# Attention on one NeuronCore: row maxima spread through DRAM by two DMAs instead of by TensorE transposes and ScalarE copies

## What is computed

```
# layer 0
xn  = group_norm(x) * gn_w + gn_b
q, k, v = split(qkv_w @ xn + qkv_b)
a   = softmax_over_keys(q . k / sqrt(64)) @ v        # per image and head, 2304 x 2304
h   = proj_w @ a + proj_b + x
# layer 1
q, k = [h, position embedding] @ Wq, Wk ;  v = h @ Wv
out = softmax_over_keys(q . k / sqrt(64)) @ v @ Wout + bout + h
```

## Time and profile before

| | |
|---|---|
| median of three runs | 4245.89 us |
| the profiled execution | 4246.06 us |
| its span in the trace | 4244.3 us |
| granted TensorE clock, mean | 0.992 |
| busy: TensorE, VectorE, ScalarE, GpSimd | 4090.6, 3200.4, 2775.9, 1408.4 us |
| attention of layer 0 and 1, first scores to about the last block | 408 to 1990 us, 2510 to 4100 us |
| DMA: bytes, mean rate | 208.42 MB, 49 GB/s |

### The profile page before, as it was taken

One profiled execution on the slowest core, in us unless ns is written; L12 is line 12 of the kernel. 1 busy time (PEld: TensorE's weight loads), 2 busy tenths in 40 slices (PEclk: granted clock), 3 DMA queues, 4 the chain that ended last, 5 costly groups with the idle time before them and its releaser, 6 DMA issues. The chain is left out here.

```text
span 4244.3 us, 88521 instructions
## 1 busy us (share of the span) xinstructions
PE 4090.6 (96%) x30024; PEld 1908.3 (45%) x30024; DVE 3200.4 (75%) x4032; ACT 2775.9 (65%) x3557; POOL 1408.4 (33%) x572
## 2 busy tenths in 40 slices
PE   7999899999999999998999989999999999999989
PEld 4554344444444444444555544444444444444445
DVE  3111899999999999997322239999999999999962
ACT  1112888888888888885000018888888888888840
POOL 0000344444444444443100004444444444444420
PEclk9999999999999999999999999999999999999999
DMA  4112000101000000011323220101000000000116
GB/s 175 74 74 93 10 27 19 37 13 32 20 28 22 22 24 24 26 49 53 117 100 126 97 95 9 30 19 33 19 28 24 22 22 26 24 20 30 41 45 215
DMA packets 157933, 208.42 MB, mean 49 GB/s; under 512 B 9008, under 2 KB 144304, under 8 KB 156848
## 3 DMA queue, kind: packets, MB, share of 16 engines
q1 hardware_dynamic: 137712, 179.28, 12.8%
q10 hardware_dynamic: 20160, 28.32, 1.8%
HBM read 113.19 MB, written 94.37 MB: 49 GB/s over the span
## 5 line engine op out<-in xcount | busy, mean ns | idle before, releaser
L589 POOL TENSOR_TENSOR prob<-prob,mx 128x1056 f32<-128x1056 f32 x564 | 1387.4, 2460 | 2627.5 <-DVE prob L589 2627.5
L753 ACT ACTIVATE prob<-psum_att 128x768 f32<-128x768 f32 x1728 | 1364.5, 822 | 951.7 <-PE psum_att L683 538.0
L683 PE MATMUL psum_att<-qst,kst 64*128 64x384 f32 x6912 | 1289.0, 505 | 30.6 <-DMA kst<-qk_scratch 18.0
L769 ACT ACTIVATE prob<-prob 128x1152 f32<-128x1152 f32 x1152 | 1291.2, 1172 | 17.3 <-POOL prob L589 15.1
L858 DVE TENSOR_TENSOR run<-psum_att,run 128x768 f32<-128x768 f32 x1344 | 1233.8, 950 | 36.1 <-PE psum_att L683 34.6
L694 PE MATMUL psum_att<-prob,vst 128*32 128x384 f32 x13824 | 1242.1, 491 | 0.7 <-ACT prob L769 0.5
L683 PEld LDWEIGHTS psum_att<-qst,kst 64*128 64x128 f32 x6912 | 623.6, 188 | 534.0 <-ACT prob L753 101.4
L589 DVE TENSOR_TENSOR prob<-prob,mx 128x1248 f32<-128x1248 f32 (+1 forms) x576 | 850.7, 1478 | 0.0
L694 PEld LDWEIGHTS psum_att<-prob,vst 128*32 128x32 f32 x13824 | 394.6, 109 | 755.3 <-issue 703.7
L870 DVE TENSOR_TENSOR two_tiles<-prob 128x768 f32<-128x768 f32 x564 | 565.3, 1002 | 1.1 <-ACT prob L769 1.1
L309 PE MATMUL psum<-xc_l,wq 128*128 128x384 f32 x1536 | 504.6, 490 | 9.3 <-DVE xc_l L382 4.4
(11 more groups left out here) (55 smaller groups left out, 1593.9 us busy)
## 6 DMA issues: line engine op xcount, KB each, us to landing
qk_scratch<-qk_l SPq DMA_DIRECT2D x48, 768.0 KB, 3.5
v_scratch<-vo_l SPq DMA_DIRECT2D x24, 768.0 KB, 3.5
qst<-qk_scratch SPq DMA_DIRECT2D x96, 192.0 KB, 2.4
kst<-qk_scratch SPq DMA_DIRECT2D x96, 192.0 KB, 2.4
vst<-v_scratch SPq DMA_DIRECT2D x96, 192.0 KB, 2.5
att_scratch<-ob ACTq DMA_DIRECT2D x96, 192.0 KB, 1.9
attc_l<-att_scratch SPq DMA_DIRECT2D x24, 768.0 KB, 5.7
x_sb<-in_x SPq DMA_DIRECT2D x8, 1152.0 KB, 14.0
```

The source lines that it names most:

```text
L589: return engine.tensor_tensor(x, x, m, ALU.subtract)
L683: mm = nc.tensor.matmul(psum[:, 2 * k + e, 0:CH], kst[rows, (3 * c + k) * P:(3 * c + k + 1) * P], qst[par][rows, :], start=True, stop=True ...
L753: nc.scalar.activation(prob[par][:, :, s, :], s_banks(k)[:, :, 0:CH], ACT.Copy).then_inc(copied, 1)
L769: nc.scalar.activation(x, x, ACT.Exp, scale=SCALE).then_inc(exp_done, 1)
```

## The change

The six broadcasting transposes and the three copies of a block go. In their place SyncE stores `mcol` to a DRAM scratch `max_scratch` (2 parities x 2 heads x 3 x 128 values; in DRAM the six values of a partition lie apart, so that each 4-byte value is a piece of its own), waits for the store, and loads the 768 values into all 128 partitions of `mx` (3 KB each). VectorE's and GpSimd's first subtraction of a block waits for that load (`mx_in`). Besides: `turn` stands behind the scores of c = 0, not ahead of them; `reduce` waits no more for scores; `pair_tiles` is done for the group 11 back at a group's start, not for the group 10 back at its end; the loops of SyncE are written out so that the first pair of heads is apart.

```diff
-SHIFT_LAG, EXP_LAG, PAIR_LAG, PV_LAG = 8, 9, 10, 11
-TURN_AT, BROADCAST_AT = 0, 1
+SHIFT_LAG, EXP_LAG, PAIR_LAG, PV_LAG = 8, 9, 11, 11
+TURN_AT = 0
...
+            def spread_max(t, par, n):
+                sp.wait_ge(reduced, 3 * (t + 1))
+                sp.dma_start(max_d[par].rearrange("e r p -> p e r"), mcol[:, :, :],
+                             allow_slow_non_contiguous=True).then_inc(mx_stored[par], 16)
+                sp.wait_ge(mx_stored[par], 16 * n)
+                sp.dma_start(mx[par][:, :, :].rearrange("p e q -> p (e q)"),
+                             max_d[par].rearrange("e r p -> (e r p)").partition_broadcast(P)).then_inc(mx_in[par], 16)
...
+                    if not before(t, 2) and j != 2:
+                        spread_max(t - 2, j % 2, pair * (JB // 2) + j // 2)
                     if j == 0:
                         for c in range(KC):
                             sp.wait_ge(scored, scored_count(slot(t - 1, 3 * c + 2)))
...
                     if j == 1:
                         for c in range(KC):
...
+                            if c == 0:
+                                spread_max(t - 1, 0, pair * (JB // 2) + 1)
...
             def bank_free(t, c, k):
                 if c > 0 or not before(t, 1):
                     pe.wait_ge(copied, slot(t, 3 * (c - 1) + k) if live(t) else slot(NB - 1, KT - 1))
-                if c == BROADCAST_AT + 1 and not before(t, 1) and live(t - 1):
-                    pe.wait_ge(mx_ready, 3 * (t - 1) + k + 1)
...
-                    if c == TURN_AT and not before(t, 1) and live(t - 1):
-                        bank_free(t, c, 2)
-                        turn(t - 1)
-                    if c == BROADCAST_AT and not before(t, 1) and live(t - 1):
-                        bank_free(t, c, 2)
-                        broadcast_max(t - 1)
...
                             scores(t, par, c, k)
+                    if c == TURN_AT and not before(t, 1) and live(t - 1):
+                        bank_free(t, c, 2)
+                        turn(t - 1)
...
-                        if c == BROADCAST_AT and not before(t, 1) and live(t - 1):
-                            copy_max(t - 1, 1 - par, k)
...
-                        pool.wait_ge(mx_ready, 3 * (t + 1))
+                        pool.wait_ge(mx_in[par], 16 * (t // 2 + 1))
...
-            def reduce(t, r):
+            def reduce(t, par, r):
                 dve.wait_ge(turned, t + 1)
-                if live(t + 1):
-                    dve.wait_ge(scored, scored_count(slot(t + 1, 3 * TURN_AT + r)))
                 if not before(t, 1):
-                    dve.wait_ge(broadcast, t)
+                    dve.wait_ge(mx_stored[1 - par], 16 * ((t - 1) // 2 + 1))
...
-                    dve.wait_ge(mx_ready, 3 * (t + 1))
+                    dve.wait_ge(mx_in[par], 16 * (t // 2 + 1))
...
                 for c in range(KC):
+                    tp, pp, cp = behind(t, par, c, PAIR_LAG)
+                    if live(tp) and not last(tp):
+                        pair_tiles(tp, pp, cp)
                     for k in range(3):
...
-                    tp, pp, cp = behind(t, par, c, PAIR_LAG)
-                    if live(tp) and not last(tp):
-                        pair_tiles(tp, pp, cp)
                     ts, ps, cs = behind(t, par, c, SHIFT_LAG)
...
+    max_d = dram("max_scratch", (2, 2, TT, P))
```

More of the change, by code:

```diff
@@ L511, in _, with attention_stage @@
                 pair(it)
-def attention_stage(nc, name, psum, bufs, qk_d, v_d, att_d, next_loads):
+def attention_stage(nc, name, psum, bufs, qk_d, v_d, att_d, max_d, next_loads):
     with ExitStack() as ctx:
@@ L538, in attention_stage @@
         reduced = sem("reduced")
-        broadcast = sem("broadcast")
-        mx_ready = sem("mx_ready")
+        mx_stored = [sem(f"mx_stored{p}") for p in range(2)]
+        mx_in = [sem(f"mx_in{p}") for p in range(2)]
         dve_shifted, pool_shifted = sem("dve_shifted"), sem("pool_shifted")
@@ L601, in _, with loads @@
         def _(sp):
-            with sp.Fori(0, B) as b, sp.Fori(0, PAIRS) as hp:
+            def spread_max(t, par, n):
[5 more added lines that the diff above has]
+                             max_d[par].rearrange("e r p -> (e r p)").partition_broadcast(P)).then_inc(mx_in[par], 16)
+            def loads(b, hp):
                 pair = b * PAIRS + hp
@@ L624, in _ @@
                                 .rearrange("(a p) d -> p a d", p=P)).then_inc(v_in[c], 16)
+                            if c == 0:
+                                spread_max(t - 1, 0, pair * (JB // 2) + 1)
+            loads(0, 0)
+            for b in range(B):
+                with sp.Fori(1 if b == 0 else 0, PAIRS) as hp:
+                    loads(b, hp)
+            for t in range(NB - 2, NB):
+                spread_max(t, t % 2, t // 2 + 1)
             for p in range(2):
@@ L637, in bank_free @@
                     pe.wait_ge(copied, slot(t, 3 * (c - 1) + k) if live(t) else slot(NB - 1, KT - 1))
-                if c == BROADCAST_AT + 1 and not before(t, 1) and live(t - 1):
-                    pe.wait_ge(mx_ready, 3 * (t - 1) + k + 1)
-                if c > BROADCAST_AT + 1 and not live(t) and live(t - 1):
-                    pe.wait_ge(mx_ready, 3 * t)
             def spare_free(t, c):
@@ L654, in turn @@
                 mm.then_inc(turned, 1)
[L656 to L662, removed]
             def turn_den(t):
@@ L753, in copy @@
                 nc.scalar.activation(prob[par][:, :, s, :], s_banks(k)[:, :, 0:CH], ACT.Copy).then_inc(copied, 1)
[L755 to L762, removed]
             def exponential(t, par, c, e):
@@ L838, in _ @@
         def _(dve):
-            def reduce(t, r):
+            def reduce(t, par, r):
                 dve.wait_ge(turned, t + 1)
-                if live(t + 1):
-                    dve.wait_ge(scored, scored_count(slot(t + 1, 3 * TURN_AT + r)))
                 if not before(t, 1):
-                    dve.wait_ge(broadcast, t)
+                    dve.wait_ge(mx_stored[1 - par], 16 * ((t - 1) // 2 + 1))
+                if r == 0 and not before(t, 2):
+                    dve.wait_ge(dve_shifted, group(t - 2, KC - 1))
+                    dve.wait_ge(pool_shifted, group(t - 2, KC - 1))
                 nc.vector.tensor_reduce(mcol[:, :, r], s_banks(r)[:, :, CH:512], AX.X, ALU.max).then_inc(reduced, 1)
@@ L906, in body @@
                 for c in range(KC):
+                    tp, pp, cp = behind(t, par, c, PAIR_LAG)
+                    if live(tp) and not last(tp):
+                        pair_tiles(tp, pp, cp)
                     for k in range(3):
                         if c == TURN_AT and not before(t, 1) and live(t - 1):
-                            reduce(t - 1, k)
+                            reduce(t - 1, 1 - par, k)
                         if c == DEN_TURN_AT and k > 0 and not before(t, 3) and live(t - 3):
@@ L991, in attention @@
                         "ones": ones, "ident": ident}
-                attention_stage(nc, f"att{layer}", psum, bufs, qk_d, v_d, att_d, next_loads)
+                attention_stage(nc, f"att{layer}", psum, bufs, qk_d, v_d, att_d, max_d, next_loads)
         def semaphores(c1, stage, n):
```

## The result

The changed kernel takes **4693.7 us** (median; 4690.03 to 4705.35) against 4245.98 of the kernel before on the same chip: a ratio of 1.106, 95% interval 1.104 to 1.108. It is 448 us slower, where 78 us faster was forecast, in a range up to 4300.

The account below looks back on a forecast made before the run. TensorE sets the pace, VectorE right behind. Of 1.44 us a block saved, 0.61 goes to a new wait; 0.83 less in 94 blocks is 78 us, so 4246.06 - 78 = 4168 us, range 4110 to 4300.

Parts of the forecast that it names:

- What bounds the kernel, and what goes from TensorE's path: TensorE sets the pace, VectorE right behind; broadcast (0.80) and fold wait (0.58) go, with small gaps 1.44 us a block.
- turn_den's new wait: In each block TensorE gives back 0.61 us, as turn_den waits for ScalarE's copy of slot 8.
- No row shows a store of 4-byte pieces ... High end: 11.4: Chain through DRAM, third reduce to shift of c = 2: 4.6 to 11.4 us, about 6.6 taken, hidden.
- The store term: SyncE's store of the maxima to DRAM: 1.9 us plus 1.3 for the pieces' packets.
- The load: SyncE's load of the maxima from DRAM into all partitions: 2.4 + 0.6 us, near to kst's.
- the 10.7 allowed: Time from the third reduce's end to the shift of c = 2, within which the DRAM chain is hidden: 10.7 us.
- The chain is late: Rival: past 11.0 us each microsecond of DRAM chain costs one a block; at 14 us, 4450 us; chance 0.10.
- pair_tiles behind shift, costed at nothing: On VectorE the pair follows the shift and gets the port before GpSimd; the swap costs nothing, pairs stay at 0.95.
- The condition on which it rests: The pair must start before GpSimd's subtraction, by 0.16 us, and GpSimd end 0.2 before the next shift.
- T + 1.53: GpSimd's start in a group, T being the start of VectorE's shift; the pair starts at T + 1.37.
- the 2.9: Sign of being right: GpSimd's (POOL's) rows at 2.9 us, with pairs at 0.95.
- SyncE's queue, ScalarE's copies, fill and drain at nothing: SyncE's new waits and ScalarE's three copies to mx cost nothing; fill and drain zero, give or take 5 us.

Follow-up runs that it names:

- E1: The changed kernel without the store of the maxima and its wait; SyncE loads 3 KB of another tensor instead, so maxima are wrong: 4162.6 us.
- E7: The changed kernel with one small transpose turning the 128 x 6 maxima into 6 rows, stored as 6 pieces of 512 bytes: 4169.9 us.
- E3: The changed kernel with the 768 pieces of 4 bytes stored 512 bytes apart in DRAM; the loaded maxima are wrong: 4175.1 us.
- E8: The changed kernel with the 768 pieces of 4 bytes stored 64 bytes apart in DRAM; the loaded maxima are wrong: 4176.5 us.
- E9: E6 with pair_tiles back ahead of the shift, for the group 10 back at a group's end: 4184.1 us.
- E6: The changed kernel with the turn taking every third column, so the store writes 256 pieces of 12 bytes: 4182.5 us.
- E10: E7 with each pair_tiles waiting for the signal of the shift ahead of it, which takes away its 0.16 us lead: 5371.7 us.
- E2: The changed kernel with a partition's six values stored side by side, 128 pieces of 24 bytes; maxima land at wrong queries: 4171.8 us.

## Why the prediction was wrong

**What bounds the kernel, and what goes from TensorE's path: right.** Without the store the time is 4162.6; my 4168 was for a kernel whose chain is hidden, and its steps (block 31.63, turn_den's new wait 0.61) were met within 0.1 us by E1. E7, which has a hidden chain and computes the same result as the changed kernel, takes 4169.9.

**"No row shows a store of 4-byte pieces ... High end: 11.4": wrong, and the step that failed.** The store term was 3.2 us and measured 10.3; even its high end, 5.3, was half of it. Both ends took 1.9 us, from issue to landing, from a store of full rows, and added for the pieces nothing but packets' times on the DMA engines (1.3, or 3.4 at the high end). The packets took 7 ns each, less than my 27; but the wait for the store ended 9.5 us after the last packet in the spread shown above, and for that time there is no row in a kernel that never writes small pieces side by side. E3 and E8, with the pieces apart, bring it down to 2.1 to 2.2 us, so it is the crowding that the sum had at nothing. "Nearest row" led astray because the rows near in size (vst's packets) were loads, and none was a write into shared units. A bound from rows that lack the mechanism is no bound; the range should have said so.

**The load: 3.0, measured 5.0** behind the clogged store, 3.4 behind none (E1). This term was short too, but within the 5.7 of the high end. The one chain followed above took 15.2 us in place of 6.6, against the 10.7 allowed; with the store at its forecast 3.2 even a load of 5.0 would have been hidden.

**"The chain is late" rival: this is what happened, with its slope too flat.** It had a chance of 0.10, low for a term that no row priced. It was forecast at one microsecond a block for each one late, and 4450 us at a chain of 14. By that slope the chain of 15.2, 4.2 past 11.0, would have made 4168 + 4.2 x 94 = 4563 us, and the 3.98 that VectorE did wait 4542. What is left, 131 to 152 us or 1.4 to 1.6 a block, is about the price of the low clock, 1.5 in the block above, which no term had. The trace before has such a case, at the start of layer 0, with the stop and, in the second view, the clock behind it:

```profile
453.21 4.21 PE L683 MATMUL psum_att<-qst,kst 64*128 64x384 f32 x12 [3.31 <-ACT prob L753]
```
```profile
453.00:456.00 3.00, 2.79 (x10) 0.50 0.02 5
```

Behind a stop of 3.31 us the clock was 0.50 and twelve score matmuls took 4.21 in place of 2.21 us. So the price of a stop could have been read, and the rival given a steeper slope.

**pair_tiles behind shift, costed at nothing: right.** 564 pairs of 952 ns, E9 equal to E6. The condition on which it rests was right too (E10). GpSimd's rows of 3.10 where I had 2.9 are no slower subtraction: its start at T + 1.53 and its end at T + 4.63 already made 3.10, and the 2.9 was a row in which it started later. The Trainium skill (SBUF — State Buffer, SBUF: two separate sides) has the loser of the port blocked for the whole of the other's instruction. By that rule, E10 agrees: the pair ends at 1013.57, 0.81 behind GpSimd's end at 1012.76.

**SyncE's queue, ScalarE's copies, fill and drain at nothing: right** as far as E1 shows, where what is left between 4168 and 4162.6 is 5 us. In the changed kernel itself the drain is not at nothing: from the last turn of layer 0 to the end of its last work it is 52.0 us, against 46.1 in E1.

## What to carry to other kernels

A DMA's time has two parts, packets and landing, and a dependent load pays both: before a small store stands in a chain, ask how many separate pieces it writes side by side, and give each partition a run (E2, E6), make each row one piece (E7), or put the pieces 64 bytes apart (E8). Measure a chain by taking out one link and leaving the rest, as E1 did: that tells what the rest is worth, here within 9 to 14 us of the kernels in which the link is back and hidden. And where two engines share a port, look at who arrives first and by how much; here 0.16 us decided over 1200.

## What was not expected of the hardware

- 768 writes of 4 bytes to 3 KB of DRAM take 10.3 us until they have landed, and 2.1 us when they are 64 bytes apart; at 16 bytes apart 3.0. This is the time from the store's issue to the issue of the load that waits for it.
- The packets of the slow store are gone within 2 us; then 7.4 to 10.6 us pass until the wait for it ends (for 9.5 us in the spread shown no DMA packet of the core moves), and loads behind it take 1.4 to 1.6 us longer.
- After stops of 0.97 and 1.79 us TensorE's granted clock was still 1.00; in a third, of 2.96 us, it showed 0.52, over the next 4.5 us of work 0.56, and 1.00 again behind them.
- A stationary operand read with a step of three columns loads in 202 ns, not 140 (E6, 128 x 128, float32).
